# Attention's fp32 value products issued three key blocks back to back, over nine probability buffers

## The chip, the cores and the metric

The kernel runs on one core of one Trainium2 chip. The metric is the device time of one execution in microseconds. Engines: TensorE (PE: matmuls; PEld: its weight loads), VectorE (DVE), ScalarE (ACT), GpSimd (POOL) and SyncE (SP), which issues the DMAs.

## What is computed

Four layers on x of 2 x 1024 x 512, each as x + layernorm(layer(layernorm(x))): a masked sparse product, a gated network with dequantized weights, an attention, and a routed low-rank layer. The change lies in the attention, 32 query heads on 8 key heads of width 16, causal, on 1024 tokens in each of two sequences:

```python
q = q * cos + _rotate_half(q) * sin            # k likewise; k and v repeated for 4 query heads each
scores = einsum('bhqd,bhkd->bhqk', q, k) / math.sqrt(HEAD_DIM)
masked = where(causal, scores, NEG)
chunk_max = padded.reshape(b, N_HEADS, s, n_chunks, CHUNK).max(axis=-1)      # CHUNK = 16
_, topk_idx = jax.lax.top_k(chunk_max, k_top)                                # k_top = 8
...
allowed = causal & (tok_mask | init_mask | recent_mask)  # chosen chunks, first 128, last 128 keys
attn = jax.nn.softmax(where(allowed, scores, NEG), axis=-1)
out = einsum('bhqk,bhkd->bhqd', attn, v)
```

## The kernel before

A hand-written schedule; every wait is on a semaphore, and each engine runs its own list in program order. The attention (L1097 on) treats 16 groups: one of 2 sequences times one of 8 key heads, each with its 4 query heads. A group has 8 **steps**, one for each tile of 128 queries; tile i needs key blocks 0 to i. `ORDER = [7, 0, 4, 3, 6, 1, 5, 2]` (L1113) is the order of the tiles, and two steps make a **unit**: (7,0), (4,3), (6,1), (5,2). Each pair holds nine key blocks. A pair of steps is in several stages at once in neighbouring units (`stages`, L1198): front (scores and choice) in unit u, mid (mask turned) in u + 1, back (masked scores, exponents, value products) in u + 2, end (the rest of the sums' copying) in u + 3.

The work of the stages:

- `score` (L1322): TensorE, bf16, one query head against up to 512 keys into one of three score banks (L1331), with the causal part added by a 128-column matmul (L1334). VectorE reduces each bank to maxima of chunks (L1485), then takes the best eight (L1492) and marks the dropped chunks (L1495 to L1532). A score waits until the bank three scores back is reduced.
- `turn_q`, `turn_k`, `turn_mask` (L1295, L1306, L1318): transposes on TensorE; ScalarE copies their results (L1411, L1412, L1406, L1417).
- `masked_score` (L1337): for one key block, the scores of 4 heads at once with the mask as extra rows, 128 x 512, into one of two back banks (L1345; L1348 or L1351 add the diagonal parts). ScalarE takes the exponent (L1423) into one of **four** buffers `probs`.
- `weigh` (L1354), called **value product** here: the probabilities of one key block times its values, fp32, 4 matmuls of 32 output columns at the column positions 0, 32, 64, 96 (L1362), one for each head, into `sums`, one of two banks. TensorE records each fp32 matmul as two passes.
- `keep_sums` (L1425): ScalarE copies the finished sums of a step to `ot` (L1427). `close` (L1366) turns them (L1373), VectorE divides (L1459, L1465), a DMA stores.

`schedule(t, u)` (L1202) writes the order of a unit for TensorE and ScalarE alike: each item gets a place between 0 and 1, and the items are sorted by it. Masked scores and value products form one list with evenly spaced places, a product two key blocks behind its masked score (`lag = 2`). The last three products of a unit have no masked score between them. VectorE and GpSimd run the steps in order.

`over_units` (L1242) runs 4 units, a loop of 8 units that turns seven times, and 8 units at the end; 64 units hold value products, 9 each.

## Time and profile before

| | us |
|---|---|
| median of 3 runs | 1647.44 (1645.67 to 1648.11) |
| profiled execution, its span | 1644.6 |
| attention, in the trace | about 690 to 1462 |
| turns of its loop end at (TensorE, L1249) | 825.6, 921.6, 1017.2, 1112.2, 1207.8, 1303.3, 1398.9 |
| busy over the span: TensorE, VectorE, ScalarE | 1432.1, 1095.3, 837.8 |

The span is the profiled execution's time from its first to its last instruction; the runs' times lie 2.8 us above it at the median. Starts are counted from the span's start. "A <- B: total, times, longest" in a view of waits reads: engine and line A stood idle until B released it. The chain that ended last covers the final layer only and says nothing of the attention. Lines of the kernel are written L1362. A TensorE row "x8" of L1362 is one value product: four matmuls of two passes each. The durations of matmul rows overlap, so what one costs is read from the distance of starts.

### The profile page before, as it was taken

The numbers are of one execution on the slowest core, as the hardware profiler recorded it, in microseconds if no ns is written. First come the engines' busy times: TensorE is split into PE (matmuls) and PEld (weight loads), VectorE is DVE, ScalarE is ACT, GpSimd is POOL, SyncE is SP. The second block draws the span as 40 slices with busy tenths as digits, with TensorE's granted clock in tenths as the row PEclk, the third lists the DMA queues.
The fourth block names the chain that finished last, engine by engine and source line by source line (L and its number), as shares of the span: only waits on it lengthen the run. The fifth ranks groups of instructions, "written<-read, shape, count | busy, mean of one in ns | idle before, by whom it ended". The sixth has DMA issues, their size and how long they took to land. (4 is left out here: it accounts for less than half of the span.)

```text
span 1644.6 us, 36918 instructions
## 1 busy us (share of the span) xinstructions
PE 1432.1 (87%) x10714; PEld 725.8 (44%) x10809; DVE 1095.3 (67%) x3636; ACT 837.8 (51%) x1562; POOL 404.5 (25%) x1251
## 2 busy tenths in 40 slices
PE   6969699999999799399989898998989899977766
PEld 3424244444444355245544454554545455443344
DVE  4786453544543369588878687887878788825556
ACT  2423441423312057367767676776767678750043
POOL 2240000000000233243334343333334333311121
PEclk9985799999999899779999999999999999998988
DMA  9400000000000035711101111110111110011111
GB/s 362 111 0 1 0 1 1 0 0 0 0 0 1 3 96 153 215 37 36 36 7 36 35 36 37 36 36 7 36 34 36 38 36 12 9 46 38 26 39 64
DMA packets 77982, 69.70 MB, mean 42 GB/s; under 512 B 44438, under 2 KB 62870, under 8 KB 77788
## 3 DMA queue, kind: packets, MB, share of 16 engines
q1 hardware_dynamic: 77788, 67.32, 13.0%
q8 instruction: 97, 1.59, 0.4%
q14 instruction: 97, 0.79, 0.2%
HBM read 36.90 MB, written 19.92 MB: 35 GB/s over the span
## 5 line engine op out<-in xcount | busy, mean ns | idle before, releaser
L1485 DVE TENSOR_REDUCE arena<-bank 128x32 f32<-128x512 f32 (+3 forms) x768 | 399.0, 551 | 124.2 <-PE bank L1331 55.4
L1423 ACT ACTIVATE arena<-bank 128x512 f32<-128x512 f32 x576 | 330.2, 604 | 146.1 <-PE bank L1345 88.6
L1331 PE MATMUL bank<-arena 96*128 96x512 bf16 (+3 forms) x768 | 250.1, 345 | 40.6 <-issue 27.0
L1362 PE MATMUL bank<-arena 128*32 128x128 f32 x4608 | 243.2, 286 | 2.9
L1345 PE MATMUL bank<-arena 123*128 123x512 bf16 x576 | 216.7, 392 | 11.3 <-ACT arena L1423 7.3
L754 PE MATMUL bank<-arena 128*128 128x512 f16 (+1 forms) x704 | 168.1, 381 | 0.0
L199 POOL TENSOR_TENSOR arena<-arena 128x1 f32<-128x1 f32 x64 | 12.3, 192 | 583.0 <-DVE arena L195 582.5
L1581 POOL TENSOR_SCALAR arena<-arena 128x128 bf16<-128x128 bf16 x384 | 144.2, 376 | 43.4 <-DVE arena L1531 19.3
L763 PE MATMUL bank<-arena 128*128 128x512 f32 (+1 forms) x352 | 152.7, 593 | 1.6 <-DVE arena L876 1.6
L1362 PEld LDWEIGHTS bank<-arena 128*32 128x32 f32 x4608 | 97.3, 108 | 127.8 <-issue 82.9
L815 ACT ACTIVATE arena<-bank 128x512 f32<-128x512 f32 (+1 forms) x88 | 52.5, 597 | 173.7 <-PE bank L751 173.6
L1331 PEld LDWEIGHTS bank<-arena 96*128 96x128 bf16 x768 | 71.5, 99 | 133.2 <-issue 70.9
L193 DVE BATCH_NORM_STATS2 arena<-bank 128x6 f32<-128x512 f32 x48 | 33.4, 696 | 138.2 <-PE bank L763 79.1
L872 DVE SCALAR_TENSOR_TENSOR arena<-bank,arena 128x512 f32<-128x512 f32 (+1 forms) x88 | 65.8, 750 | 88.6 <-PE bank L754 87.6
L1569 POOL TENSOR_TENSOR arena<-arena 128x4 f32<-128x4 f32 x128 | 25.7, 201 | 401.4 <-DVEq L1503 401.3
L1417 ACT ACTIVATE arena<-bank 27x1024 bf16<-27x1024 bf16 (+1 forms) x128 | 102.9, 804 | 33.6 <-PE bank L1318 31.3
L1334 PE MATMUL bank<-arena 128*128 128x128 bf16 x512 | 114.0, 226 | 0.0
L754 PEld LDWEIGHTS bank<-arena 128*128 128x128 f16 (+1 forms) x704 | 70.3, 100 | 83.6 <-issue 2.5
L763 PEld LDWEIGHTS bank<-arena 128*128 128x128 f32 (+1 forms) x352 | 66.3, 190 | 85.5 <-issue 83.3
L1492 DVE MAX8 arena<-arena 128x8 f32<-128x48 f32 (+7 forms) x512 | 98.0, 191 | 5.2
L1648 PE MATMUL bank<-arena 128*128 128x512 f32 x128 | 63.5, 654 | 22.0 <-DVE arena L219 21.7
L1412 ACT ACTIVATE arena<-bank 96x512 bf16<-96x512 bf16 x128 | 79.3, 619 | 2.6 <-PE bank L1295 2.6
(217 smaller groups left out, 2276.9 us busy)
## 6 DMA issues: line engine op xcount, KB each, us to landing
arena<-qk_rows SPq DMA_DIRECT2D x16, 960.0 KB, 5.1
qk_rows<-arena SPq DMA_DIRECT2D x16, 768.0 KB, 4.1
arena<-arena SPq DMA_DIRECT2D x32, 256.0 KB, 3.0
arena<-in_x SPq DMA_DIRECT2D x4, 1024.0 KB, 12.7
out<-arena SPq DMA_DIRECT2D x16, 256.0 KB, 2.0
qk_rows<-arena SPq DMA_DIRECT2D x16, 192.0 KB, 4.7
arena<-in_down_q SPq DMA_DIRECT2D x1, 2752.0 KB, 16.6
arena<-in_up_q SPq DMA_DIRECT2D x1, 2560.0 KB, 18.9
```

The lines of the kernel that those rows point to most:

```text
L754: last = pe.matmul(m.banks[k][0:r, :], W[k][:, dc * INNER + i * P:dc * INNER + i * P + r], part[:, dc * G * P:(dc + 1) * G * P], start=par ...
L763: last = pe.matmul(m.banks[6 + t % 2][:, :], m.f32(HT_AT + i * D + t * P, P)[0:r, :], m.f32(WD_AT + i * D, D)[0:r, :], start=i == 0, stop= ...
L1331: last = pe.matmul(bank[:, 0:k1 - k0], query_aug[st.slot][0:ROWS, h * P:(h + 1) * P], key_aug[st.p][0:ROWS, k0:k1], start=True, stop=not d ...
L1334: last = pe.matmul(bank[:, k1 - k0 - P:k1 - k0], m.ident_bf, m.causal, start=False, stop=True)
L1345: last = pe.matmul(bank[:, :], key_aug[st.p][0:KROWS, j * P:(j + 1) * P], query_aug[st.slot][0:KROWS, f * N:(f + 1) * N], start=True, stop ...
L1362: last = pe.matmul(sums[st.k % 2][32 * h:32 * h + 32, :], v_staged[st.p][:, j * 32:(j + 1) * 32], probs[u % 4][:, h * P:(h + 1) * P], star ...
L1412: act.activation(query_aug[st.slot][0:ROWS, 0:N], turn_bf[0:ROWS, 0:N], ACT.Copy).then_inc(top_kept, 1)
L1417: act.activation(query_aug[st.slot][ROWS:KROWS, 0:n], turn_bf[ROWS:KROWS, 0:n], ACT.Copy).then_inc(mask_kept, 1)
L1423: act.activation(probs[u % 4], back_bank[u % 2][:, :], ACT.Exp, scale=float(HD) ** -0.5).then_inc(probs_ready, 1)
L1485: dve.tensor_reduce(out=cm[:, h * 64 + k0 // CHUNK:h * 64 + k1 // CHUNK], in_=score_bank[bank_of_score(front, number)][:, 0:k1 - k0].rearr ...
L1492: dve_seq.mark(dve.max(out=tp[:, h * TOPK:(h + 1) * TOPK], in_=chunks(cm, h)))
L1581: last = pool.tensor_scalar(out=chunk_diag[st.slot][:, h * P:(h + 1) * P], in0=m.ident_bf, scalar1=own_dropped[p4][:, h:h + 1], scalar2=NE ...
```

## The change

Value products are issued in bursts of three key blocks (`BURST = 3`) with one wait for the last tile's exponents; each still counts its own `summed`. `probs` has nine buffers (`PROBS = 9`), and the head start of `summed` is nine. Masked scores are placed at n / 10.5, the bursts at 4.7 / 10.5 = 0.448, 7.7 / 10.5 = 0.733 and 0.985 of a unit. Both steps' sums are copied at 0.05 and 0.12 of the next unit; before, the first step's were copied within the unit, behind its last product. Four groups of buffers (`v_staged`, `own`, `ot`, `o_staged`) move to free space, to make room. Line numbers in the changed kernel are lower by 4 to 6 in this part: L1362 is L1358, L1331 is L1325, L1345 is L1339, L1318 is L1312.

```diff
+    spare = m.taker(LWORK, ARENA - SEQ)
+    BURST, PROBS = 3, 9
-    probs = [take(N) for _ in range(4)]
+    probs = [take(N) for _ in range(PROBS)]
...
-        backs = []
-        lag = 2
-        for n in range(len(tiles) + lag):
-            if n < len(tiles):
-                backs.append(("masked", *tiles[n]))
-            if n == 1 and end:
-                backs.append(("sums", end[1], 0))
-            if n >= lag:
-                backs.append(("weigh", *tiles[n - lag]))
-                if tiles[n - lag] == (back[1], 0):
-                    backs.append(("sums", back[0], 0))
-        if not back and end:
-            backs = [("sums", end[1], 0)]
+        backs = [(n / (len(tiles) + 1.5), ("masked", *tile)) for n, tile in enumerate(tiles)]
+        for first in range(0, len(tiles), BURST):
+            at = min((first + BURST + 1.7) / (len(tiles) + 1.5), 0.985)
+            backs.append((at, ("burst", tiles[first:first + BURST], 0)))
+        backs += [(f, ("sums", st, 0)) for f, st in zip((0.05, 0.12), end)]
...
-        places += [(n / max(len(backs), 1), x) for n, x in enumerate(backs)]
+        places += backs
...
-            def weigh(st, j):
-                u = back_at[st.at] + j
-                if j == 0:
-                    pe.wait_ge(ot_ready, st.n + 1)
-                    if st.at == 0:
-                        pe.wait_ge(v_in[st.p], st.q * 16 + 16)
-                pe.wait_ge(probs_ready, st.g * BK + (u + 3))
...
+            def weigh(tiles):
+                done, at = tiles[-1][0], tiles[-1][1]
+                pe.wait_ge(probs_ready, done.g * BK + (back_at[done.at] + at + 3))
+                for st, j in tiles:
+                    u = back_at[st.at] + j
...
+                                         probs[u % PROBS][:, h * P:(h + 1) * P], start=j == 0, stop=j == st.i, tile_position=(0, 32 * h))
+                    last.then_inc(summed, 1)
```

Below, `d_probs` is the semaphore of finished exponents, `d_reduced` that of reduced score banks, `d_mask`, `d_minus` and `d_mask_kept` those of the mask's parts and its copy, `d_ot` that of copied sums, `d_diag` that of the dropped chunks' diagonal. TensorE in the middle of unit (7,0), before:

```order
L1334 MATMUL bank<-arena 128x128
L1362 MATMUL bank<-arena 32x128 [waits d_probs,d_ot]
L1362 MATMUL bank<-arena 32x128 x3
L1330 REGISTER_ALU
L1331 MATMUL bank<-arena 128x512 [waits d_reduced]
L1342 REGISTER_ALU
L1345 MATMUL bank<-arena 128x512 [waits d_probs]
L1292 REGISTER_ALU
L1295 MATMUL bank<-arena 96x128 [waits d_top_kept]
L1295 MATMUL bank<-arena 96x128 x3
L1362 MATMUL bank<-arena 32x128 [waits d_probs]
L1362 MATMUL bank<-arena 32x128 x3
```

The same engine in the same unit, in the changed kernel, at its first burst:

```order
L1325 MATMUL bank<-arena 128x512 [waits d_reduced]
L1306 REGISTER_ALU
L1307 REGISTER_ALU [waits d_mask_kept]
L1312 MATMUL bank<-arena 27x128 [waits d_mask,d_minus]
L1312 MATMUL bank<-arena 27x128 x7
L1358 MATMUL bank<-arena 32x128 [waits d_ot,d_probs]
L1358 MATMUL bank<-arena 32x128 x11
L1324 REGISTER_ALU
L1325 MATMUL bank<-arena 128x512 [waits d_reduced]
```

The single products between scores are gone; twelve matmuls (three products) stand behind the eight mask turns in one piece, and the next score behind them.

TensorE at the end of unit (4,3), before:

```order
L1348 MATMUL bank<-arena 128x512
L1362 MATMUL bank<-arena 32x128 [waits d_probs,d_ot]
L1362 MATMUL bank<-arena 32x128 x3
L1313 REGISTER_ALU [waits d_mask_kept]
L1318 MATMUL bank<-arena 27x128 [waits d_mask,d_minus]
L1318 MATMUL bank<-arena 27x128 x3
L1360 REGISTER_ALU
L1362 MATMUL bank<-arena 32x128 [waits d_probs]
L1362 MATMUL bank<-arena 32x128 x3
L1360 REGISTER_ALU
L1362 MATMUL bank<-arena 32x128 [waits d_probs]
L1362 MATMUL bank<-arena 32x128 x3
```

And there in the changed kernel:

```order
L1307 REGISTER_ALU [waits d_mask_kept]
L1312 MATMUL bank<-arena 27x128 [waits d_mask,d_minus]
L1312 MATMUL bank<-arena 27x128 x3
L1350 REGISTER_ALU
L1358 MATMUL bank<-arena 32x128 [waits d_ot,d_probs]
L1358 MATMUL bank<-arena 32x128 x11
L1324 REGISTER_ALU [waits d_top_kept]
L1325 MATMUL bank<-arena 128x512 [waits d_reduced]
```

Three products stood together there before too, each with its own wait for its exponents; now they share one. Counted over four units, with products and mask turns that touch as one, TensorE's list has 32 narrow blocks before (9, 7, 9, 7) and 16 in the changed kernel (4, 3, 5, 4).

## Rows read from the trace of the kernel before

**Rows 1.** The page: busy time of each engine; costliest groups of instructions
```profile
PE 1432.1 (87%) x10714; PEld 725.8 (44%) x10809; DVE 1095.3 (67%) x3636; ACT 837.8 (51%) x1562; POOL 404.5 (25%) x1251
...
L1423 ACT ACTIVATE arena<-bank 128x512 f32<-128x512 f32 x576 | 330.2, 604 | 146.1 <-PE bank L1345 88.6
...
L1362 PEld LDWEIGHTS bank<-arena 128*32 128x32 f32 x4608 | 97.3, 108 | 127.8 <-issue 82.9
```

**Rows 2.** Windows, two loop turns: length, PE, PEld, DVE, ACT, POOL busy, clock
```profile
923.00:1018.00 95.00, 87.29 (x1016) 44.84 (x1028) 76.17 (x327) 69.38 (x132) 34.60 (x127) 0.96 0.09 32
1018.00:1113.00 95.00, 87.32 (x1016) 44.94 (x1028) 76.44 (x328) 69.37 (x132) 34.98 (x129) 0.96 0.10 32
```

**Rows 3.** Windows of units (4,3), (6,1), (5,2), (7,0), and their sum
```profile
1037.21:1048.15 10.94, 10.47 (x129) 5.41 (x129) 10.07 (x47) 8.47 (x17) 4.40 (x18) 1.00 0.01 3
1048.15:1059.21 11.06, 10.71 (x134) 5.58 (x132) 9.16 (x37) 8.90 (x17) 4.28 (x15) 1.00 0.16 45
1059.21:1069.71 10.50, 10.38 (x125) 5.38 (x126) 9.47 (x43) 8.56 (x18) 4.40 (x18) 1.00 0.22 88
1069.71:1080.83 11.12, 11.03 (x132) 5.66 (x131) 9.33 (x39) 8.58 (x17) 4.38 (x16) 1.00 0.01 3
sum 43.62, PE 42.59 PEld 22.03 DVE 38.03 ACT 34.52 POOL 17.46; mean PE 10.65 PEld 5.51 DVE 9.51 ACT 8.63 POOL 4.37
```

**Rows 4.** Waits from 1030 to 1111 us: total, times, longest
```profile
DVE arena L1485 <- PE bank L1334: 6.0, 16, 0.9
...
PEld bank L1331 <- DVE arena L1485: 4.5, 14, 0.6
PEld bank L1362 <- ACT arena L1423: 4.1, 14, 0.4
...
PE bank L1331 <- DVE arena L1485: 1.1, 4, 0.3
DVE arena L1485 <- PE bank L1331: 0.8, 2, 0.4
```

**Rows 5.** Timeline of TensorE, a lone product: start, duration, line
```profile
1003.33 0.39 PE L1345 MATMUL bank<-arena 123*128 123x512 bf16 x1
1003.56 0.38 PE L1348 MATMUL bank<-arena 128*128 128x512 bf16 x1
1003.87 0.43 PE L1362 MATMUL bank<-arena 128*32 128x128 f32 x8
1004.23 0.28 PE L1331 MATMUL bank<-arena 96*128 96x256 bf16 x1
```

**Rows 6.** Timeline of TensorE, what follows a 128-column matmul
```profile
1043.00 0.22 PE L1334 MATMUL bank<-arena 128*128 128x128 bf16 x1
1043.06 0.38 PE L1345 MATMUL bank<-arena 123*128 123x512 bf16 x1
...
1044.67 0.22 PE L1334 MATMUL bank<-arena 128*128 128x128 bf16 x1
1044.82 0.43 PE L1362 MATMUL bank<-arena 128*32 128x128 f32 x8
```

**Rows 7.** Timelines of narrow windows in three products in a row, then PEld's
```profile
1016.58 0.27 PE L1362 MATMUL bank<-arena 128*32 128x128 f32 x1
...
1016.61 0.56 PE L1362 MATMUL bank<-arena 128*32 128x128 f32 x7
...
1017.10 0.16 PEld L1362 LDWEIGHTS bank<-arena 128*32 128x32 f32 x8 [0.19 <-ACT arena L1423]
```

**Rows 8.** Timeline of TensorE, a product and eight mask turns
```profile
1041.08 0.42 PE L1362 MATMUL bank<-arena 128*32 128x128 f32 x8
1041.34 0.61 PE L1318 MATMUL bank<-arena 128*27 128x128 bf16 x8
1041.88 0.39 PE L1345 MATMUL bank<-arena 123*128 123x512 bf16 x1
```

**Rows 9.** VectorE's waits in the units (4,3), (6,1), (5,2), (7,0)
```profile
DVE arena L1485 <- PE bank L1334: 0.3, 1, 0.3
...
DVE arena L1485 <- PE bank L1334: 1.0, 3, 0.4
...
DVE arena L1485 <- PE bank L1331: 0.4, 1, 0.4
DVE arena L1485 <- PE bank L1334: 0.4, 1, 0.4
...
DVE arena L1485 <- PE bank L1334: 1.0, 3, 0.6
```

**Rows 10.** Timeline of VectorE: a reduction, the best eight, the next step's first reductions
```profile
1045.67 0.69 DVE L1485 TENSOR_REDUCE arena<-bank 128x32 f32<-128x512 f32 x1
1046.28 0.42 DVE L1492 MAX8 arena<-arena 128x8 f32<-128x32 f32 x2
...
1048.15 2.21 DVE L1485 TENSOR_REDUCE arena<-bank 128x32 f32<-128x512 f32 x4
```

**Rows 11.** Groups of instructions from 660 to 1500 us: copies of the sums
```profile
L1427 ACT ACTIVATE arena<-bank 128x128 f32<-128x128 f32 x128 | 36.3, 283 | 1.2 <-PE bank L1362 0.4
```

**Rows 12.** Timeline of TensorE, first matmuls after two turns of the loop
```profile
1021.22 0.60 PE L1331 MATMUL bank<-arena 96*128 96x512 bf16 x2 [3.69 <-issue]
...
1117.03 0.79 PE L1331 MATMUL bank<-arena 96*128 96x512 bf16 x2 [4.49 <-issue]
```

More of the change, by code:

```diff
@@ L1116, in attention @@
     staged = [take(ST_W, BF16) for _ in range(2)]
-    v_staged = [take(SEQ_TILES * 32) for _ in range(2)]
-    probs = [take(N) for _ in range(4)]
+    v_staged = [spare(SEQ_TILES * 32) for _ in range(2)]
+    probs = [take(N) for _ in range(PROBS)]
     W = [take(GQ * 2 * (MASK_ROWS + 1), BF16) for _ in range(SEQ_TILES)]
@@ L1122, in attention @@
     top = [take(GQ * TOPK) for _ in range(4)]
-    own = [take(GQ * CPT) for _ in range(4)]
+    own = [spare(GQ * CPT) for _ in range(4)]
     own_dropped = [take(GQ) for _ in range(4)]
@@ L1126, in attention @@
     minus_rest = [take(GQ) for _ in range(2)]
-    ot = [take(P) for _ in ORDER]
+    ot = [spare(P) for _ in ORDER]
     inverse = [take(4 * GQ) for _ in range(CLOSES)]
-    o_staged = [take(SEQ_TILES * GQ * HD) for _ in range(2)]
+    o_staged = [spare(SEQ_TILES * GQ * HD) for _ in range(2)]
     neg_one, one_row = take(GQ), take(GQ)
@@ L1153, in attention @@
     RING = SC + CLOSES
-    assert RING % 3 == 0 and BK % 4 == 0
+    assert RING % 3 == 0 and BK % PROBS == 0 and BK % 2 == 0
     PAIR = 2 * SEQ_TILES
@@ L1279, in _ @@
                     load_rows(t * 2 + (2 + p), p)
-                    sp.wait_ge(summed, t * 2 * BK + ((p + 1) * BK + 4))
+                    sp.wait_ge(summed, t * 2 * BK + ((p + 1) * BK + PROBS))
                     load_v(t * 2 + (2 + p), p)
@@ L1352, in masked_score @@
                 last.then_inc(masked_scored, 1)
-            def weigh(st, j):
-                u = back_at[st.at] + j
-                if j == 0:
-                    pe.wait_ge(ot_ready, st.n + 1)
-                    if st.at == 0:
-                        pe.wait_ge(v_in[st.p], st.q * 16 + 16)
-                pe.wait_ge(probs_ready, st.g * BK + (u + 3))
-                for h in range(GQ):
-                    last = pe.matmul(sums[st.k % 2][32 * h:32 * h + 32, :], v_staged[st.p][:, j * 32:(j + 1) * 32],
-                                     probs[u % 4][:, h * P:(h + 1) * P], start=j == 0, stop=j == st.i, tile_position=(0, 32 * h))
-                last.then_inc(summed, 1)
+            def weigh(tiles):
[3 more added lines that the diff above has]
+                    u = back_at[st.at] + j
+                    if j == 0:
+                        pe.wait_ge(ot_ready, st.n + 1)
+                        if st.at == 0:
+                            pe.wait_ge(v_in[st.p], st.q * 16 + 16)
+                    for h in range(GQ):
+                        last = pe.matmul(sums[st.k % 2][32 * h:32 * h + 32, :], v_staged[st.p][:, j * 32:(j + 1) * 32],
+                                         probs[u % PROBS][:, h * P:(h + 1) * P], start=j == 0, stop=j == st.i, tile_position=(0, 32 * h))
+                    last.then_inc(summed, 1)
             def close(t, u):
@@ L1387, in body @@
                         masked_score(st, n)
-                    elif stage == "weigh":
-                        weigh(st, n)
+                    elif stage == "burst":
+                        weigh(st)
                     elif stage == "close":
@@ L1422, in exponent @@
                 act.wait_ge(summed, st.g * BK + (u + 1))
-                act.activation(probs[u % 4], back_bank[u % 2][:, :], ACT.Exp, scale=float(HD) ** -0.5).then_inc(probs_ready, 1)
+                act.activation(probs[u % PROBS], back_bank[u % 2][:, :], ACT.Exp, scale=float(HD) ** -0.5).then_inc(probs_ready, 1)
             def keep_sums(st):
-                act.wait_ge(summed, st.g * BK + (back_at[st.at + 1] + 4))
+                act.wait_ge(summed, st.g * BK + (back_at[st.at + 1] + PROBS))
                 act.activation(ot[st.slot], sums[st.k % 2], ACT.Copy).then_inc(ot_ready, 1)
@@ L1551, in _ @@
             pool.memset(neg_one, -1.0).then_inc(w_blank, 1)
-            pool.sem_inc(summed, 4)
+            pool.sem_inc(summed, PROBS)
             for p in range(2):
```

## The prediction, made before the result

> **What bounds the kernel now.** I read the page's busy shares first: TensorE 87%, VectorE 67%, ScalarE 51% of the span [rows 1]. These are averages over seven stages, so next come the windows of the attention loop, one per turn of eight units: in a turn of 95 us TensorE is busy 87.3, VectorE about 76, ScalarE 69 [rows 2]. Then four units in the middle of a turn, where the clock is granted in full: 43.62 us, TensorE 42.59, VectorE 38.03, ScalarE 34.52 [rows 3]. A busy TensorE need not be at its peak, so the waits matter: over 81 us its weight loads wait 4.5 us for VectorE's reductions (1.1 more on the matmul side), 4.1 us for the exponents before a value product, and little else [rows 4]. VectorE waits 6.0 + 0.8 us for score matmuls there. So TensorE is the bound for most of the time, with VectorE close behind: of the four units it is idle for 0.87, 1.90, 1.03 and 1.79 us [rows 3]. What TensorE gives back counts only until VectorE is full. That is the frame of the sum.
>
> **What a value product costs now.** A value product is four fp32 matmuls, one for each 32-column group of the array, each recorded as two passes: eight records. Between two full-width matmuls of 512 columns the starts are 0.23 us apart (1003.33, 1003.56); from the second one to the first pass of a value product it is 0.31 (1003.87); from there to the next full-width matmul 0.36 (1004.23) [rows 5]. So entry costs 0.31 - 0.22 = 0.09 us. After a 128-column matmul it is the same: 0.15 (1044.67 to 1044.82) where full width follows after 0.06 (1043.00 to 1043.06) [rows 6]. A lone product thus costs 0.36 + 0.09 = 0.45 us.
>
> **What one costs behind another.** The trace has this only at the ends of units, where three products follow in a row. In the column group that was held up by the mask turns, four passes (two products) start from 1016.58 to 1016.90: the last of the seven records ends 1017.17 and one pass takes 0.27. That is three steps of 0.11 us, so 0.22 us for a product [rows 7]. A burst of three costs 0.36 + 2 x 0.22 = 0.80, with its entry 0.89, against 1.35 for three lone ones. Each narrow block that is merged into another saves 0.45 - 0.22 = 0.23 us.
>
> **How many are merged.** The mask turns (27 columns) are narrow too and share a block with a product beside them: product at 1041.08, eight turns from 1041.34, full width again at 1041.88, which is 0.80 = 0.36 + 8 x 0.055, so no second switch [rows 8]. Counted with them in the program order, narrow blocks per unit go from 9 to 4 in unit (7,0), 7 to 3 in (4,3), 9 to 5 in (6,1), 7 to 4 in (5,2): 32 to 16 in four units, not 36 to 12 as the bursts alone would suggest. In two of the four units the third product in a row also waits 0.19 us for its exponents [rows 7]; afterwards the last tile's exponents are placed at 0.76 of the unit and the burst at 0.985, so this wait goes. TensorE gives back: (7,0) 5 x 0.23 = 1.15 us; (4,3) 4 x 0.23 + 0.19 = 1.11; (6,1) 0.92; (5,2) 3 x 0.23 + 0.19 = 0.88. Sum 4.06 us in four units.
>
> **What of that reaches the end.** VectorE can't be quicker than its own work. Upper bound: the smaller of TensorE's gift and VectorE's idle time in each unit, 1.15 + 0.87 + 0.92 + 0.88 = 3.8 us. But part of the idle time is only the gap between a dependent pair of VectorE instructions. The named waits for score matmuls are 1.0 us in (7,0), 0.3 in (4,3), 1.0 in (6,1) and 0.8 in (5,2) [rows 9]; the smaller of gift and named wait gives 1.0 + 0.3 + 0.92 + 0.8 = 3.0 us. From this comes off what the burst itself adds: it keeps TensorE away from scores for 0.80 us in place of 0.36, so a score that VectorE waits for behind it comes 0.44 us later. VectorE has up to two filled banks of 0.69 us each in hand, and most of the bursts at the end of a unit lie beside its choosing of chunks, which takes 1.9 us (1046.28 to 1048.15) [rows 10], so I count one exposed burst in four units: 3.0 - 0.44 = 2.6 us. There are 64 units with value products (576 products, nine a unit [rows 1]), 16 times four: 41 us. The ends for this term are 61 us (3.8 x 16) and below nothing (the slower rival).
>
> **The other edits.** Nine probability buffers in place of four: the exponent of a tile waits for the product nine tiles back, which ended a unit earlier, so no new wait; with four buffers bursts would hold up ScalarE. No memory traffic; four groups of buffers move to free space. The burst waits for its third tile's exponents, and queued behind it on TensorE are scores and masked scores; the third tile is issued 1.7 slots (about 1.8 us) ahead, and an exponent takes 0.60 us [rows 1], so it is covered; uncovered it would cost up to 0.4 us, the longest such wait now [rows 4]. The sums' copies (128 of them, 0.28 us [rows 11]) only move, to 0.05 and 0.12 of the next unit: the products that overwrite the banks come at 0.45, the transposes that need them at 0.37 or later, so nothing waits. ScalarE has 9 us free in four units [rows 3]. SP's load of the values waits for the same product; the count it waits for only grows by the larger head start. At each turn of the loop TensorE stands 3.7 to 4.5 us [rows 12]; the changed loop body is shorter by some address arithmetic and I see no reason for another price, but even the same code varies by 0.8 us here, so six turns may bring 5 us either way.
>
> The sum: span 1644.6 - 41 = 1603.6, plus the 2.8 us between the profiled span and the median of the runs (1647.4): **1606 us**.
>
> **Rivals.** *More than the forecast*: VectorE's small gaps close too. For it speaks that 5.6 us of idle stand in four units [rows 3], against it that only 3.1 us of them are put down to TensorE. It gives 48 to 61 us, 1586 to 1599. *Bursts expose scores*: a third of the 24 bursts of a turn, not 2, hold back a score that VectorE waits for: 8 x 0.44 = 3.5 of the 6.0 us (3.0 x 2) are lost, 2.5 x 8 = 20 us are left, 1627. For it: in unit (7,0) eight mask turns and a burst follow on one score, 0.09 + 0.45 + 0.80 = 1.3 us, about as much as the two banks in hand. *Slower*: the same mechanism, at the scores behind the bursts of all units. It decides from 6.0 / 0.44 = 14 exposed bursts in 24; with 18 of them 7.9 - 6.0 = 1.9 us are added in each turn, 15 us in all, 1662. Against it: the choosing follows six of the eight score groups and covers a burst. *It doesn't do what it says*: if in a burst each pass had to wait for its weights to load (0.108 us mean [rows 1]), a step would be 0.22 in place of 0.11 us, the burst 0.36 + 4 x 0.22 = 1.24, with entry 1.33 against 1.35: nothing given back, 1645 to 1649. The four evenly spaced starts in rows 7 speak against it, but they are of one column group only.
>
> That last rival is also what a page of the Trainium skill would have. "TensorE: Matmul & The Clock Gate", Part 3, "The mechanism", states that a weight load overlaps with matmuls in flight only when their row groups differ; all these products use all 128 rows. By it the change would give nothing; by rows 7 it gives 0.23 us a block.
>
> **How the numbers follow.** Forecast (1600 to 1620) 0.50; more than that (1580 to 1600) 0.15; exposed bursts (1620 to 1643) 0.20; no saving 0.05; slower 0.10. The range that leaves out 0.2 is 1585 to 1640: it holds the forecast's case, 0.12 of the larger gain's 0.15 and 0.18 of the exposed bursts' 0.20; what is below needs loop turns that are shorter besides. A measurement of this kernel can tell about 0.2% (3.3 us) from no change; beyond it, faster has 0.85 (0.50 + 0.15 + 0.20), slower 0.10, and 0.05 stay within.
>
> **What would show it.** Lone narrow blocks gone from TensorE's timeline, bursts 0.80 us from first pass to next full-width matmul; the four units down from 43.6 to about 41.0 us; TensorE's waits for L1485 up from 5.6 us in 81, and VectorE's waits for scores down from 6.8 to about 2. If VectorE's waits stay and TensorE's fall, the bursts expose scores. If a burst takes 1.2 us, the weight loads are in the way. If the four units shrink as foretold and the whole doesn't, it is the turns of the loop. The forecast is wrong if VectorE's busy time per unit is above 9.5 us afterwards.

## The result, and the profile after

The change makes the kernel faster, by about a quarter of what was forecast: 1636.53 us at the median of 4 runs (1635.81 to 1637.74), beside 1647.78 for the kernel before on the same chip. The ratio is 0.9928, with a 95% interval of 0.9913 to 0.9943. The profiled execution spans 1635.9 us. The forecast was 1606 us, 41 us less; 11 us came.

In this part of the changed kernel L1331 is L1325, L1334 is L1328, L1345 is L1339, L1362 is L1358, L1295 is L1289, L1411 and L1412 are L1407 and L1408, L1423 (exponent) is L1419, L1427 (copy of the sums) is L1423, L1373 is L1369 and L1485 is L1481. The page of the changed kernel, busy time and groups, to be read beside [rows 1]:

```profile
PE 1401.3 (86%) x10713; PEld 748.6 (46%) x10809; DVE 1087.5 (66%) x3636; ACT 827.3 (51%) x1562; POOL 404.0 (25%) x1251
...
L1481 DVE TENSOR_REDUCE arena<-bank 128x32 f32<-128x512 f32 (+3 forms) x768 | 396.0, 549 | 119.6 <-PE bank L1328 58.0
L1419 ACT ACTIVATE arena<-bank 128x512 f32<-128x512 f32 x576 | 335.7, 610 | 178.3 <-PE bank L1339 103.7
```

TensorE is busy 31 us less than before, and the whole is 9 us shorter in the two profiles. TensorE has gained idle time as well as shed work. The same four units as in [rows 3], in the windows of the changed kernel (columns as in rows 2):

```profile
1031.60:1042.20 10.60, 9.74 (x127) 5.55 (x127) 9.91 (x47) 8.22 (x16) 4.40 (x19) 1.00 0.02 5
1042.20:1053.20 11.00, 10.37 (x136) 6.26 (x136) 8.90 (x37) 9.18 (x18) 4.30 (x15) 1.00 0.22 68
1053.20:1064.10 10.90, 9.97 (x122) 5.36 (x123) 9.43 (x43) 8.22 (x16) 4.34 (x18) 1.00 0.15 61
1064.10:1075.10 11.00, 10.31 (x130) 6.07 (x130) 9.26 (x40) 8.22 (x16) 4.45 (x16) 1.00 0.01 3
sum 43.50, PE 40.38 PEld 23.24 DVE 37.50 ACT 33.84 POOL 17.49; mean PE 10.10 PEld 5.81 DVE 9.38 ACT 8.46 POOL 4.37
```

The four units take 43.5 us, as before (43.62), and were foretold at 41.0. Only the idle time of TensorE grew, from 1.0 to 3.1 us. What it waits for stands in the view of waits, 1026 to 1107 us. That is 81 us from 12 us behind a turn of the loop, placed as [rows 4] is; a window that starts nearer to the turn takes in what the turn does:

```profile
DVE arena L1481 <- PE bank L1328: 6.0, 12, 0.8
PEld bank L1339 <- ACT arena L1419: 5.4, 18, 0.5
PEld bank L1325 <- DVE arena L1481: 5.2, 18, 0.4
...
PEld bank L1289 <- ACT arena L1408: 3.9, 7, 0.8
...
PEld bank L1358 <- ACT arena L1419: 2.8, 7, 0.5
...
PE bank L1289 <- ACT arena L1408: 1.9, 5, 0.5
DVE arena L1481 <- PE bank L1325: 1.8, 6, 0.4
PE bank L1358 <- ACT arena L1419: 1.4, 4, 0.4
...
PE bank L1339 <- ACT arena L1419: 0.5, 2, 0.3
```

The weight loads of masked scores now wait 5.4 us for ScalarE's exponents, where this wait was 0.4 us before:

```profile
PEld bank L1345 <- ACT arena L1423: 0.4, 1, 0.4
```

A masked score goes into one of two back banks, and that bank must have been read by the exponent two key blocks back. The turns of queries (L1289) wait 3.9 us for ScalarE's copy of the last turn, against 1.2 before (L1295 there). The PE rows are not to be added to these: they tell of the same moments, and only of what was left when the matmuls ahead had run out. Before, the only such row was 1.1 us for VectorE [rows 4]. Now all three are for ScalarE, 1.9, 1.4 and 0.5 us, and what each is worth only experiments can say. VectorE's waits for scores rose from 6.8 to 7.8 us, and TensorE's for VectorE's reductions, added up as the prediction did it, went from 5.6 to 5.2.

The burst itself costs what was forecast. TensorE's timeline of the changed kernel, a burst (x24: three products of eight records) and the matmul behind it:

```profile
1070.88 0.38 PE L1339 MATMUL bank<-arena 123*128 123x512 bf16 x1
1071.19 0.86 PE L1358 MATMUL bank<-arena 128*32 128x128 f32 x24
1071.98 0.39 PE L1339 MATMUL bank<-arena 123*128 123x512 bf16 x1
```

0.31 us to its first pass, then 0.79 to the next full-width matmul. Of the bursts whose 24 records stand in one piece, with a 512-column matmul behind them without a wait, there are 137 in the trace, 0.795 us at the median; 0.80 was worked out.

Where most of the 11 us come from shows at the turns of TensorE's loop. Before, TensorE stands still twice there: 3.69 us of idle time behind the branch [rows 12], and once more a few matmuls on, a row of the kernel before that was not shown:

```profile
1024.28 0.59 PE L1345 MATMUL bank<-arena 123*128 123x512 bf16 x1 [1.97 <-issue]
```

In the changed kernel, the same places behind the turn at 1013.8:

```profile
1017.80 1.03 PE L1325 MATMUL bank<-arena 96*128 96x512 bf16 x2 [3.30 <-issue]
...
1019.16 0.31 PE L1289 MATMUL bank<-arena 128*96 128x128 bf16 x1
1020.55 0.48 PE L1289 MATMUL bank<-arena 128*96 128x128 bf16 x3 [1.07 <-issue]
```

As distances between starts of matmuls, the two stalls are 7.05 us a turn before (4.78 + 2.27, mean of six) and 5.21 after (3.59 + 1.63). Six turns of 1.84 us are 11.0 us, about the whole gain. Counted as idle time of TensorE, without the ordinary spacing of matmuls, it is 6.15 and 4.63 us a turn, 9 us in six. So the question for the experiments is twofold: why do the stalls differ, and who eats the 2.6 us in four units that the bursts should give.

### The profile page after: what moved, and what is told of

Its sections match the earlier page's. It is cut to its first block and busy times, and to the rows that moved or that the text cites. A ratio compares the mean times of both kernels' runs of the same rounds, so it can differ in the third digit from the quotient of the medians.

```text
span 1635.9 us, 36841 instructions
## 1 busy us (share of the span) xinstructions
PE 1401.3 (86%) x10713; PEld 748.6 (46%) x10809; DVE 1087.5 (66%) x3636; ACT 827.3 (51%) x1562; POOL 404.0 (25%) x1251
## 5 line engine op out<-in xcount | busy, mean ns | idle before, releaser
L1481 DVE TENSOR_REDUCE arena<-bank 128x32 f32<-128x512 f32 (+3 forms) x768 | 396.0, 549 | 119.6 <-PE bank L1328 58.0
L1419 ACT ACTIVATE arena<-bank 128x512 f32<-128x512 f32 x576 | 335.7, 610 | 178.3 <-PE bank L1339 103.7
L1325 PE MATMUL bank<-arena 96*128 96x512 bf16 (+3 forms) x768 | 248.8, 348 | 27.1 <-issue 19.9
L1339 PE MATMUL bank<-arena 123*128 123x512 bf16 x576 | 225.4, 396 | 10.7 <-ACT arena L1419 7.2
L1358 PE MATMUL bank<-arena 128*32 128x128 f32 x4608 | 171.7, 277 | 12.6 <-ACT arena L1419 12.4
L1577 POOL TENSOR_SCALAR arena<-arena 128x128 bf16<-128x128 bf16 x384 | 144.2, 376 | 43.3 <-DVE arena L1527 19.1
L1358 PEld LDWEIGHTS bank<-arena 128*32 128x32 f32 x4608 | 120.1, 110 | 43.0 <-ACT arena L1419 24.7
L1325 PEld LDWEIGHTS bank<-arena 96*128 96x128 bf16 x768 | 72.0, 100 | 117.1 <-DVE arena L1481 51.0
L1328 PE MATMUL bank<-arena 128*128 128x128 bf16 x512 | 114.2, 225 | 0.0
L1339 PEld LDWEIGHTS bank<-arena 123*128 123x128 bf16 x576 | 56.1, 100 | 83.2 <-ACT arena L1419 47.6
```

Source lines behind the costliest of these rows:

```text
L1325: last = pe.matmul(bank[:, 0:k1 - k0], query_aug[st.slot][0:ROWS, h * P:(h + 1) * P], key_aug[st.p][0:ROWS, k0:k1], start=True, stop=not d ...
L1328: last = pe.matmul(bank[:, k1 - k0 - P:k1 - k0], m.ident_bf, m.causal, start=False, stop=True)
L1339: last = pe.matmul(bank[:, :], key_aug[st.p][0:KROWS, j * P:(j + 1) * P], query_aug[st.slot][0:KROWS, f * N:(f + 1) * N], start=True, stop ...
L1358: last = pe.matmul(sums[st.k % 2][32 * h:32 * h + 32, :], v_staged[st.p][:, j * 32:(j + 1) * 32], probs[u % PROBS][:, h * P:(h + 1) * P], ...
L1419: act.activation(probs[u % PROBS], back_bank[u % 2][:, :], ACT.Exp, scale=float(HD) ** -0.5).then_inc(probs_ready, 1)
L1481: dve.tensor_reduce(out=cm[:, h * 64 + k0 // CHUNK:h * 64 + k1 // CHUNK], in_=score_bank[bank_of_score(front, number)][:, 0:k1 - k0].rearr ...
```

## The experiments

| run | median us | ratio to before, 95% | four units | stalls a turn |
|---|---|---|---|---|
| before | 1647.8 | | 43.6 | 7.05 |
| after | 1636.5 | 0.9928 (0.9913 to 0.9943) | 43.5 | 5.21 |
| e1_nine_buffers | 1646.7 | 0.9998 (0.9989 to 1.0008) | 43.6 | 7.0 |
| e2_burst_of_one | 1667.3 | 1.0127 (1.0110 to 1.0143) | 45.2 | 5.8 |
| e3_one_copy_back | 1626.6 | 0.9880 (0.9863 to 0.9896) | 42.8 | 5.4 |
| e6_code_moved_24 | 1630.1 | 0.9891 (0.9873 to 0.9909) | 43.5 | 3.5 |
| e4_half_exponents | 1600.2 | 0.9714 (0.9685 to 0.9742) | 41.1 | 5.2 |
| e7_before_unrolled | 1595.8 | 0.9688 (0.9666 to 0.9711) | 43.5 | none |
| e8_after_unrolled | 1599.1 | 0.9706 (0.9684 to 0.9728) | 43.6 | none |
| e9_bursts_old_places | 1661.0 | 1.0086 (1.0063 to 1.0110) | 45.1 | 5.1 |
| e5_half_reductions | 1627.1 | 0.9868 (0.9843 to 0.9892) | 43.2 | 5.0 |
| e10_before_half_exponents | 1646.5 | 0.9995 (0.9985 to 1.0005) | 43.3 | 6.9 |
| e11_one_copy_back_unrolled | 1590.4 | 0.9652 (0.9627 to 0.9677) | 42.9 | none |
| e12_second_copy_late | 1605.6 | 0.9741 (0.9721 to 0.9760) | 44.0 | none |
| e16_three_back_banks | 1618.1 | 0.9832 (0.9816 to 0.9848) | 42.1 | 5.1 |
| e17_three_back_banks_unrolled | 1576.7 | 0.9581 (0.9563 to 0.9599) | 42.1 | none |
| e18_burst_of_one_half_exponents | 1649.5 | 1.0017 (1.0007 to 1.0027) | 44.1 | 6.1 |

Runs are compared by their ratios to the kernel before, since not all were on one chip together. "Four units" is the time of (4,3), (6,1), (5,2) and (7,0) where no turn of the loop lies between. It is the safer measure of the two: behind each turn TensorE's granted clock is at its lower level for a time that differs between the profiled runs, 41 us over the six turns in the kernel before, 51 in the changed one, 58 in e10, and the whole time takes that in.

### The parts of the change alone

The kernel before, in its own order, with nine buffers (`PROBS = 9`) and the moved groups:

```diff
-    probs = [take(N) for _ in range(4)]
+    probs = [take(N) for _ in range(PROBS)]
```

> The kernel before with nine probability buffers and the four buffer groups moved, its order of work unchanged. Theory L (all of the 11 us gained comes from the six turns of TensorE's loop, whose stalls fell from 7.0 to 5.2 us each because the loop's code stands elsewhere and is shorter): code as long and as placed as before, so 1647 us within 2. Theory S (part of the gain is in the steady units, from the buffers): up to 5 us faster. Both expect four units of 43.6 us.

1646.7 us, the same as before. The buffers and their places cost and give nothing.

The changed kernel with the new places but single products:

```diff
-    BURST, PROBS = 3, 9
+    BURST, PROBS = 1, 9
```

> The changed kernel with bursts of one product, everything else as changed (places by the same rule, nine buffers, sums copied at the head of the next unit). Narrow blocks rise from 4, 3, 5, 4 to 9, 7, 10, 8 a unit, 18 more in four units, so TensorE has 18 x 0.23 = 4.1 us more to do in four units that last 43.5. Theory H (the bursts pay, but the moved copies and places cost as much at the heads of the units): four units take about 46 us, the whole about 1670 us. Theory D (VectorE's waits behind bursts eat the gift, places and copies cost nothing): four units as before, 43.6 us, the whole 1636 to 1648 depending on the loop's turns.

1667.3 us. Against e1 the new places, those of the sums' copies included, cost 1.6 us in four units; two more narrow blocks than before (34 for 32) are in it, 0.5 us by the price of the prediction. Against this run the bursts give 1.7 to 1.8 back (45.2 to 43.5). So the change is two things: an order that is worse, and a saving that pays for it. The order's cost was not in the sum at all.

Bursts with everything else at its old place in the order (the burst where its third product stood, each sums' copy where it was):

```diff
-                backs.append(("weigh", *tiles[n - lag]))
+                if (n - lag) % BURST == BURST - 1:
+                    order.append(("burst", tiles[n - lag - BURST + 1:n - lag + 1], 0))
```

> Nine buffers and bursts of three, but masked scores and copies of the sums at the places of the kernel before; each burst stands where its third product stood. 14 narrow blocks in four units in place of 32, so TensorE has 18 x 0.23 = 4.1 us less to do. Theory H (the new places and the copies at the unit's head cost what the bursts gave): four units about 41.5 us (43.6 less 2), the whole with loop turns like the changed kernel's about 1605 us. Theory D (a burst keeps scores from VectorE wherever it stands): four units 43 to 43.6, the whole 1630 to 1638 us.

1661.0 us, worse than either kernel and outside what both theories expected. Its waits, 1036 to 1117 us, 12 us behind a turn like those above (L1493 is the reduction here, L1351 the masked score, L1431 the exponent, L1370 the value product):

```profile
PEld bank L1351 <- ACT arena L1431: 7.8, 16, 1.0
DVE arena L1493 <- PE bank L1340: 7.8, 15, 1.2
...
PEld bank L1370 <- ACT arena L1431: 3.2, 7, 0.5
```

The masked scores wait 7.8 us for exponents, in single waits of up to 1.0. The reading that fits is this, though no run takes it apart: on the old places the third product of a burst needs the exponents of a masked score only two key blocks back, as a lone one did, but now three products, with scores and masked scores behind them, stand behind that wait; the wait itself is 3.2 us in single waits of up to 0.5. Bursts at the new places last 1.6 us less in four units than at the old ones (43.5 for 45.1), though the new places cost something by themselves.

### Who holds TensorE up

The changed kernel with each exponent over half of its columns; the products read that half twice, so TensorE has the same instructions. ScalarE has 7 us less to do in four units:

```diff
-                act.activation(probs[u % PROBS], back_bank[u % 2][:, :], ACT.Exp, scale=float(HD) ** -0.5).then_inc(probs_ready, 1)
+                act.activation(probs[u % PROBS][:, 0:N // 2], back_bank[u % 2][:, 0:N // 2], ACT.Exp, scale=float(HD) ** -0.5).then_inc(probs_ready, 1)
```

> The changed kernel with each exponent taken of half the columns (256 of 512); two heads' products read the other two's probabilities, so part of the softmax is left out. ScalarE's step for an exponent falls from 0.48 to about 0.27 us, 7.5 us less in four units. Theory H (TensorE's waits for ScalarE at the heads, and the exponents between masked scores, hold the units up): four units 43.5 to about 41 us. Theory D (scores behind bursts and VectorE's own work): under 0.7 us less.

The changed kernel goes from 1636.5 to 1600.2 us. The same edit in the kernel before:

> The kernel before (its loop kept) with each exponent taken of half the columns, as was done to the changed kernel, which lost 2.4 us in four units (43.5 to 41.1) and 36 us in all. Theory N (ScalarE became a bound by the change; before, TensorE was): four units 43.6 to no less than 42.8, the whole at least 1632 us. Rival (ScalarE's latency held up the kernel before just as much): four units about 41.3, the whole about 1609 us.

1646.5 us: nothing in the whole, and 0.3 us in four units (43.6 to 43.3). And in the changed kernel with bursts of one:

> The changed kernel with bursts of one and exponents of half the columns (part of the softmax left out, as in the half-exponent run of the changed kernel, which lasted 1600 us, four units 41.1). With full exponents a burst of three saved 1.7 us in four units (45.2 to 43.5) of the 4.1 that TensorE was given. Theory R: with ScalarE light the gift comes through, so bursts of one last 44.0 to 45.0 in four units, the whole about 1650 us. Rival (VectorE's waits eat it in any case): 42.8 or less, the whole 1625 us or less.

1649.5 us. The sums of the four units' windows in e10, e18 and e4, in this order:

```profile
sum 43.30, PE 42.64 PEld 22.10 DVE 37.91 ACT 27.53 POOL 17.43; mean PE 10.66 PEld 5.52 DVE 9.48 ACT 6.88 POOL 4.36
```

```profile
sum 44.10, PE 43.15 PEld 21.40 DVE 37.87 ACT 27.59 POOL 17.32; mean PE 10.79 PEld 5.35 DVE 9.47 ACT 6.90 POOL 4.33
```

```profile
sum 41.10, PE 39.63 PEld 23.11 DVE 36.97 ACT 26.74 POOL 17.41; mean PE 9.91 PEld 5.78 DVE 9.24 ACT 6.69 POOL 4.35
```

This is the cleanest result of the study. With a light ScalarE, bursts of three in place of single products give 3.0 us in four units (44.1 to 41.1). The whole change (e10 to e4) gives 2.2 us in four units, 16 x 2.2 = 35 us, where 41 were forecast for this term. All in all it gives 46, but 10 of these are shorter stalls at the turns (6.9 to 5.2, six times), which the forecast did not have; of the 49 us between e18 and e4 such stalls are 6. With ScalarE's full work the whole change gives 0.1 in four units. So ScalarE was hardly a bound before (e10), and it is what eats the gain after: 2.1 of 2.2 us.

Is VectorE a bound too? Its reductions cut to half the columns:

```diff
-                                          in_=score_bank[bank_of_score(front, number)][:, 0:k1 - k0].rearrange("p (c d) -> p c d", d=CHUNK),
+                                          in_=score_bank[bank_of_score(front, number)][:, 0:(k1 - k0) // 2].rearrange("p (c d) -> p c d", d=CHUNK // 2),
```

> The changed kernel with each reduction of a score bank reading half of the columns (chunk maxima of 8 keys in place of 16, so the choice of chunks is another), about 10 us less work for VectorE in four units of 43.5. Theory N (ScalarE holds the units up since the change): four units 42 us or more, the whole 1612 or more. Theory D (VectorE holds them up): four units 40.5 us or less, the whole under 1590 us.

```profile
sum 43.20, PE 40.24 PEld 23.55 DVE 29.81 ACT 33.84 POOL 17.52; mean PE 10.06 PEld 5.89 DVE 7.45 ACT 8.46 POOL 4.38
```

VectorE is busy 7.7 us less, and the four units are 0.3 us shorter; the whole gains 9.5 us, 5 of them (0.3 x 16) in such units. For the rest, the profiled run has 41 us of lower clock over its six turns where the changed kernel has 51; why is open. VectorE, which the sum had as the limit, is not the one that counts here. Whether it would be the next limit, with ScalarE light too, was not run; in e4 TensorE's weight loads wait 7.7 us in 81 for its reductions.

### What of ScalarE: its work at the head of a unit, and the two back banks

The timeline of ScalarE at the head of a unit of the changed kernel, and TensorE's row that waits there:

```profile
1064.62 0.60 ACT L1419 ACTIVATE arena<-bank 128x512 f32<-128x512 f32 x1 [1.15 <-PE bank L1339]
1065.11 0.27 ACT L1423 ACTIVATE arena<-bank 128x128 f32<-128x128 f32 x1
1065.27 0.59 ACT L1407 ACTIVATE arena<-bank 96x512 bf16<-96x512 bf16 x1
1065.74 0.60 ACT L1408 ACTIVATE arena<-bank 96x512 bf16<-96x512 bf16 x1
1066.22 0.61 ACT L1419 ACTIVATE arena<-bank 128x512 f32<-128x512 f32 x1
1066.70 0.30 ACT L1423 ACTIVATE arena<-bank 128x128 f32<-128x128 f32 x1
1066.86 0.63 ACT L1419 ACTIVATE arena<-bank 128x512 f32<-128x512 f32 x1
1067.33 0.64 ACT L1408 ACTIVATE arena<-bank 96x512 bf16<-96x512 bf16 x1
```

```profile
1066.40 0.42 PE L1289 MATMUL bank<-arena 128*96 128x128 bf16 x4 [0.44 <-ACT arena L1408]
```

ScalarE has no gap for over 3 us, from 1064.62 on: exponents, two copies of turned queries and both copies of sums (L1423), 0.16 us each by the distance of starts (1065.11 to 1065.27). TensorE waits 0.44 us for the end of the copy at 1065.74. Elsewhere in the unit ScalarE stands idle now and then: it is busy for 33.84 of the 43.5 us of the four units (51% is its share of the whole span), and neither share tells where its work stands. One of the two copies moved back behind its burst, into the unit that made the sums:

```diff
+            if (back[0], back[0].i) in [(x, y) for x, y in tiles[first:first + BURST]]:
+                backs.append((at, ("sums", back[0], 0)))
-        backs += [(f, ("sums", st, 0)) for f, st in zip((0.05, 0.12), end)]
+        backs += [(0.12, ("sums", st, 0)) for st in end[1:]]
```

> The changed kernel with the first step's sums copied in its own unit again, right behind the burst that ends it; only the second step's copy stays at the head of the next unit. Theory H (ScalarE is crowded at the heads of units: TensorE's waits for its copies of the queries rose from 1.2 to 5.8 us in 81): one 0.16 us step leaves the head, TensorE's waits for L1408's copy fall by a third or more, four units 43.5 to about 42.8, the whole about 1626 us. Theory D (scores exposed behind bursts): 1635 to 1638 us, no change.

1626.6 us, 9.9 less than after, or 0.155 us for each of 64 units. From the first masked score of a unit to that of the next, each of the four units is 0.17 us shorter: one copy's length. In its waits, 1017 to 1098 us, the masked scores (L1341 here) wait as long as before the edit, and the turns of queries (L1291) less, 2.5 for 3.9:

```profile
PEld bank L1341 <- ACT arena L1421: 5.4, 18, 0.5
...
PEld bank L1291 <- ACT arena L1410: 2.5, 5, 0.7
```

Then the other copy, moved from 0.12 to 0.30 of the unit. This and the kernel that it is compared with have no turns of the loop:

```diff
-        backs += [(0.12, ("sums", st, 0)) for st in end[1:]]
+        backs += [(0.3, ("sums", st, 0)) for st in end[1:]]
```

> The kernel with bursts and one copy of the sums back in its own unit (1626.6 us with the loop), with the attention's loop written out. Four units lasted 42.8 us there against 43.5 in the changed kernel, so 16 x 0.7 = 11 us under the changed kernel written out (1599.1): 1588 us. That would be under the kernel before written out (1595.8) too. If turns and order acted on each other: 1595 us or more.

> As the kernel with one copy back, written out, and the other copy of the sums at 0.30 of the unit in place of 0.12, behind both copies of the queries. Theory H (every ScalarE step ahead of the queries' copies at the head of a unit delays TensorE): another 0.3 us in four units at least, 1583 us or less. Rival (the head holds one copy without harm): 1588 us, no change.

With the one copy back, the unrolled kernel takes 1590.4 us, near what was expected, and 5.4 less than the kernel before unrolled (e7, 1595.8). The late copy is a miss: 1605.6 us with it at 0.30. From first masked score to first masked score, unit (7,0) gains 0.16 us as the theory has it (10.68 to 10.52), but (4,3) goes from 10.56 to 11.79: there `close` turns the sums early in the unit, and TensorE's transposes (L1365 here) wait for the late copy (L1419 here), with scores behind them in TensorE's list:

```profile
1061.97 0.22 PE L1324 MATMUL bank<-arena 128*128 128x128 bf16 x1
1063.31 0.44 PE L1365 MATMUL bank<-arena 128*128 128x128 f32 x2 [1.12 <-ACT arena L1419]
```

The other half of ScalarE's hold is the ring of two back banks. A third bank, got by putting both sums side by side in one bank; both copies now wait for the unit's last product, and the next unit's first burst waits for both copies. All work is kept:

```diff
-    score_bank, back_bank, turn_bank = m.banks[0:3], m.banks[3:5], m.banks[5]
-    sums = [m.banks[6 + i][:, 0:P] for i in range(2)]
+    score_bank, back_bank, turn_bank = m.banks[0:3], m.banks[3:5] + m.banks[7:8], m.banks[5]
+    sums = [m.banks[6][:, i * P:(i + 1) * P] for i in range(2)]
```

> The changed kernel with three banks for masked scores in place of two; both sums share one bank, so both copies wait for the unit's last product and the next unit's first burst waits for both copies. Theory R (the two-bank ring is shorter than a burst, so ScalarE idles in a burst and TensorE waits for it afterwards): TensorE's waits for exponents before masked scores (4.9 us in 81) fall under 2, four units 43.5 to 42 or less, the whole about 1612 us. Rival (ScalarE's load or the places, not the ring): four units 43 or more, the whole 1630 us or more.

1618.1 us, 18.5 less than after. The waits, 1009.5 to 1090.5 us (81 us), and the four units:

```profile
PEld bank L1289 <- ACT arena L1408: 3.9, 7, 0.8
...
PEld bank L1339 <- ACT arena L1419: 0.4, 2, 0.2
```

```profile
sum 42.10, PE 39.44 PEld 22.89 DVE 37.39 ACT 33.72 POOL 17.34; mean PE 9.86 PEld 5.72 DVE 9.35 ACT 8.43 POOL 4.34
```

The masked scores' 5.4 us of waiting for exponents are 0.4 now; the turns' 3.9 us have stayed, since they hang on the copies at the unit's head. Four units are 1.4 us shorter. Of the 2.4 us that a light ScalarE gives (43.5 to 41.1), the bank gives 1.4 and one copy's place 0.6 to 0.7; the two were not run together.

### The turns of the loop

If the stalls at a turn hang on where the loop's code lies, 24 instructions put before TensorE's loop should move them without changing the loop:

```diff
+            for _ in range(12):
+                pe.transpose(turn_bf[0:ROWS, 0:P], m.ident_bf[:, 0:ROWS], m.ident_bf)
             turn_k(0, 0, 0, 0, True)
```

> The changed kernel with 12 transposes more on TensorE (24 instructions) ahead of the attention, while it waits for a DMA anyway; the loop's code is the same, 24 instructions further on. Theory L (after a turn TensorE stalls a second time about 17 instructions on, because a boundary of the code it fetches lies there): the second stall of 1.4 to 1.9 us goes or moves, the whole 1626 to 1630 us. Rival (the stall belongs to what follows the turn, the waits and the clock at 1.2 GHz): stalls as they are, 1636 to 1638 us.

1630.1 us, 6.4 less than after, although the kernel does more. TensorE's timeline behind a turn:

```profile
1013.13 1.03 PE L1325 MATMUL bank<-arena 96*128 96x512 bf16 x2 [3.23 <-issue]
...
1014.49 0.63 PE L1289 MATMUL bank<-arena 128*96 128x128 bf16 x4
1014.91 0.63 PE L1325 MATMUL bank<-arena 96*128 96x512 bf16 x1
```

The first stall stands; the second, which split the four L1289 transposes of the changed kernel at 1020.55, is gone at all six turns. The stalls are 3.49 us a turn, and turn follows turn after 92.1 us instead of 93.6. The instructions of the loop are the same, so the second stall depends on the code's position. The whole is only 6.4 us shorter though six turns give 9: in the profiles, 4.5 us are lost again behind the attention, from the last masked score to the end (188.6 us after, 193.1 here), and that was not followed up.

Then both kernels with the loop unrolled:

```diff
-        with eng.Fori(0, GROUPS // 2 - 1) as t:
+        for t in range(GROUPS // 2):
```

> The kernel before with the attention's loop written out (seven copies of its body on each engine, no branch), nothing else changed. Theory L (each turn costs TensorE 7.0 us of stall and, with the clock at 1.2 GHz behind it, the two units around it 8.3 us more than others): 6 x 8.3 = 50 us less, 1597 us; steady units as before, 43.6 us for four. Rival (long straight code stalls as often, at each boundary of what is fetched): 1640 us or more.

> The changed kernel with the attention's loop written out in the same way. Theory L: the two units around a turn last 28.7 us against 21.9 for the same pair elsewhere, so 6 x 6.8 = 41 us less than 1636: 1595 us, within 3 us of the kernel before written out (1597), since without turns nothing of the change's gain is left. Rival (the bursts gave something in the steady units): at least 6 us under the kernel before written out.

1595.8 us for before, 1599.1 for after. Both were run together, and set against each other their four times each do not overlap (1594.8 to 1596.9, 1598.7 to 1600.1): without turns the changed kernel is 3.3 us slower, a fifth of a per cent. So the gain hangs on the turns, and it is more than the 11 us: leaving the turns out takes 51 us from the kernel before and 37 from the changed one. The turns became 14 us cheaper, and 3 of these are lost elsewhere.

Last, the three back banks unrolled, the best kernel of the study:

> The same with the attention's loop written out, which took 37 us from the changed kernel. Theory R: 1612 - 37 = 1575 us, under every kernel so far. Rival: 1593 us or more.

1576.7 us, 4.2% less than before and 60 us less than after. 22 us of it are the third bank (against e8), 37 us the loop.

## Why the prediction was wrong, point by point

- **The burst's price** held: 0.795 us measured for 0.80. The rival by which weight loads would stand in the way fell; it needed 1.24. With it falls, for this case, the rule of the Trainium skill ("TensorE: Matmul & The Clock Gate", Part 3, "The mechanism") that a load overlaps only with matmuls of another row group: all of a burst's products use all 128 rows, and the passes of one column group follow each other at about 0.11 us with a load (0.110 us at the mean) for each.
- **TensorE's gift and VectorE's share** were near the right size where ScalarE is light: 3.0 us in four units for the bursts and 2.2 for the whole change with half the exponents, against 2.6 in the sum. How much of the difference is VectorE's, no run tells.
- **"What of that reaches the end" is the step that failed.** It set TensorE's gift against VectorE's idle time alone. ScalarE was let off with 9 us free in four units, a sum over the time that says nothing of the places. TensorE and ScalarE hand each other two back banks, and one bank of turned queries; where TensorE comes sooner, masked scores (5.4 us of waits for 0.4) and turns of queries (3.9 for 1.2) find ScalarE still at work. The third bank (e16) and the lighter exponents (e4) show it; the cap that belonged in the sum was the one by ScalarE's rings and copies, and with the price of the order it leaves 0.1 us of the 2.6.
- **"The sums' copies only move, so nothing waits" failed too.** The places of those who need the copies were looked at (and e12 shows that this matters, too), but not who stands behind the copies in ScalarE's list. A copy costs its 0.16 us in each unit there, 10 us in all (e3).
- **The order's own price** had no term. The new places of masked scores, products and copies cost 1.6 us in four units with single products (e2 against e1), 0.8 with a light ScalarE (e18 against e10); the copies of the point above are part of it.
- **The turns of the loop** were given no other price, 5 us either way. They gave 14 by the unrolled pair, 11 of them in the stalls. That the whole came out faster at all is luck as far as the forecast goes: the mechanism that it named gave nothing, and the turns, for which it saw no reason, gave the result. That the code is shorter was seen; that a stall can vanish with its position (e6) was not.
- **"Exposed bursts"** (1620 to 1643 us) is the rival in whose range the time fell, but by another mechanism: VectorE's waits for scores rose to 7.8 us and TensorE's for VectorE went from 5.6 to 5.2, much like the sign that the prediction gave for exposed bursts; yet e5 shows that VectorE gains little from less work, and e4 that the gain comes back through ScalarE. So that sign did not tell the two apart. Of the other signs foretold, the burst's 0.80 came; the four units' 41.0 and VectorE's fall to 2 us of waits didn't. That the four units might not shrink at all with bursts of 0.80 us was no case of the prediction; it should have been one, with ScalarE in it.

What stays open: why the first stall behind the branch is 4.8 us at the mean before and 3.6 after. The looped kernels with the new order or with bursts have the short one (3.4 to 3.8 us), e1 and e10, in the old order, the long one (4.7). The traces show what goes with it: nearly all long stalls hold two transfers of instructions, the short ones one (last section). No run separates the length of the loop's code from its position for it.

## What to carry to other kernels

When a change makes the bound engine faster, list every ring that it shares with any other engine, and ask of each whether its slots last for the new pace; an engine that is idle for a fifth of the time can still hold every slot of a ring of two when the next is wanted. Take its busy share from the stage in question and not from the page: ScalarE's was 51% of the span, but 79% of these units (34.52 of 43.62 us). Before a short piece goes onto an engine's list at a place where that engine has a run of work ahead, ask what stands behind it there, and who waits for the piece itself: here one early copy cost its whole length in every unit, and the other, moved late, cost more. And before a gain of under 1% in a looped program is put down to an edit, measure the turns of the loop apart from the body, or compare both kernels unrolled.

## What was unexpected of the hardware

A turn of TensorE's loop, whose body leaves about 2300 instruction records (2044 of them matmuls and weight loads), costs a first stall of 3.2 to 5.5 us and, in all looped kernels but e6, a second one of 1.3 to 2.9 us some 15 instructions on. The second one vanishes when the code before the loop grows by 24 instructions. The trace has the branch itself, seven times in a kernel: six times it is taken, and its record then lasts 3.7 to 5.1 us before and 3.6 to 3.8 in the changed kernel; the last time it falls through, in 0.08 us. The branches of the other engines take under 0.1 us each. Shortest, median and longest of TensorE's, in ns, before (L1249) and in the changed kernel (L1243):

```profile
L1249 PEldq COMPARE_BRANCH  x7: 83/4530/5123, 825.6 to 1398.9; - x7
```

```profile
L1243 PEldq COMPARE_BRANCH  x7: 76/3672/3797, 826.1 to 1388.5; - x7
```

The Trainium skill ("Runtime: NRT & Kernel Launch", "Instruction fetch mechanics") says that TensorE's instruction memory holds 2048 instructions, is refilled in 16 KiB blocks of 256, and that a taken branch to a target outside the window forces a fetch. The traces agree as far as they go. They have a DMA queue of the kind "instruction", q8, whose transfers are 16384 bytes each; the views do not say which engine's code it brings. One turn of the loop before, after and in e6 (921.5 to 1017.1, 921 to 1014, 917.4 to 1009.4 us):

```profile
q8 instruction: 12, 0.20, 0.9%
```

```profile
q8 instruction: 11, 0.18, 0.9%
```

```profile
q8 instruction: 10, 0.16, 0.7%
```

Within the first stall stand two of these transfers in 16 of the 18 turns of the kernels in the old order (before, e1, e10), and these stalls last 4.4 to 5.5 us; the other two hold one transfer and last 3.8 and 4.0. All other looped kernels have one there, and 3.2 to 4.1 us. The next transfer starts about 0.5 us behind the first stall, and in the changed kernel the second stall ends 1.2 to 1.5 us after that transfer has landed; e6 has this transfer too, but no stall, and it lacks the following one. So stalls and transfers go together, and the position of the code moves both; that the one causes the other is not shown. Transfers alone don't stall TensorE: the unrolled kernels (e7, e8) have 66 from 700 to 1460 us, and no turn's stall.

The stall has a tail. Behind it the granted clock is at the lower of TensorE's levels, 1.2 GHz (0.50 of 2.4), as the windows of the changed kernel show:

```profile
1017.80:1022.80 5.00, 3.92 (x14) 2.01 (x15) 2.33 (x4) 2.50 (x6) 0.00 (x0) 0.50 0.02 5
1022.80:1026.00 3.20, 3.20 (x44) 1.99 (x43) 2.58 (x6) 2.84 (x5) 0.00 (x0) 0.87 0.02 5
```

It stays there for 6.8 us behind each of the six turns in the kernel before, and behind three of the six in the changed kernel; behind its other three it stays for 10.2, as in this window, and why is open:

```profile
1109.00:1119.20 10.20, 7.15 (x32) 3.64 (x36) 4.80 (x9) 4.77 (x10) 0.48 (x2) 0.50 0.02 5
```

So a turn costs more than its stalls. Unrolling took away six turns and gave 51 us in the kernel before and 37 in the changed one, 8.5 and 6.2 us a turn, where the stalls are 7.05 and 5.21.
